# Block rounds of a two-layer decoder: inverses from ScalarE's logarithm and exponential, tables inside the first round, and new orders of smaller pieces

## The chip, the core and the metric

The kernel is one program on one core of a Trainium2 chip. Its engines run side by side and meet at semaphores: TensorE (PE; its weight loads are shown as PEld), VectorE (DVE), ScalarE (ACT), GpSimd (POOL), and SyncE, whose queue (SPq) starts most of the DMAs. The metric is the device time of one execution in microseconds (us).

## What is computed

The input is 64 sequences of 64 tokens with 256 channels, so 4096 tokens. Two layers follow each other; each has an attention part, a part that reads a context, and a feed-forward part. The change lies in the second and third part of layer 0:

```python
x = x + _L0_xattn_ref(64, 64, 256, L0_xattn_w, L0_xattn_u, _layernorm(x, axis=-1), ctx_2048)
x = x + _L0_ffn_ref(_layernorm(x, axis=-1), router_weight, router_bias, gate_up_proj, ...)   # 8 experts, best 2
```

The first of them is a recurrence over time in every channel, with key k (the normalised x) and value v (the context). Up to a common factor it is

```python
q_t = decay * q_(t-1) + exp(k_t);  p_t = decay * p_(t-1) + exp(k_t) * v_t      # decay = exp(w)
y_t = (p_(t-1) + exp(u + k_t) * v_t) / (q_(t-1) + exp(u + k_t))
```

The second normalises again, computes 8 logits per token, takes the best two, and sends the token to these two experts. The normalisation is (x - mean) / sqrt(variance + 1e-5), so every token needs the power -1/2 of a number, and every token and channel of the recurrence needs the inverse of a denominator.

## The kernel before

The kernel has four stages after each other: the linear attention of layer 0; the block rounds, which are changed here; the experts' matmuls over sorted rows; and layer 1. The block rounds and the experts are the function `recurrence_and_experts`.

**Blocks and rounds.** The 4096 tokens are 8 blocks of 512. A block goes through three steps, called f, y and r in the code. In step f its x is normalised (statistics on DVE, power -1/2 on POOL, scaling on ACT), TensorE turns keys and values to channels by time and adds the age of each time step from a small table (`aged`, `now`), and ACT takes the exponentials: `eh` of the keys, `fk` of the keys with the bonus u. POOL multiplies `eh` by the values `vt` (`ev`, function `weighted`). In step y DVE runs two scans with the decays `keep` (`qp` over `eh`, `pp` over `ev`), forms the denominator `den`, inverts it, and multiplies it by the numerator `num`, which POOL makes (functions `now_weighted`, line 1025, and `numerator`, line 1011). TensorE also makes key and value rows of the context for layer 1 (`cross_kv`, four tiles for each block, taken out by `kv_out` on ACT). In step r y is turned back and added to x (`residual`), normalised a second time (`xh`), and routed: logits, best two, their ranks in the experts' lists (`choose`, `place`), and POOL sends the rows out by indirect DMA (`scatter`, eight DMAs for each block). Weights of the experts are split into a high and a low part on the way (`weights_high` on ACT, `weights_low` on DVE, `down_high` on ACT, `down_low` on POOL).

Round i works on f of block i, y of block i-1 and r of block i-2, so there are 10 rounds (0 to 9), and rounds 2 to 7 hold all three steps. Each engine has the order of its pieces written out by hand, in a loop over `STEPS`; an engine does its pieces in that order and waits at a piece until its semaphores have come. On DVE the order is: statistics of f, `weights_low`, the router's weights of the block before, residual and statistics of r, both scans, the reciprocal (line 1412, `nc.vector.reciprocal(den[:], den[:])`), `choose`, the quotient (line 1417), `place`. On TensorE it is: tile 2 of `cross_kv` (y), `y_T` (r), tile 3 (y), `v_T` and `k_T` (f), `h_T` (r), tile 0 (f), `router` (r), tile 1 (f), `ranks` (r). In front of the loop DVE makes the tables `keep`, `aged`, `now`, and only then it starts on block 0.

**The power -1/2** is a function of POOL:

```python
def power(k, b):
    pool.wait_ge(S(f"var{k}"), 2 * b + 2)
    nc.gpsimd.tensor_tensor(out=rs[k][:], in0=ve[k][:], in1=neghalf[:], op=ALU.pow).then_inc(S(f"rs{k}"), 1)
    pool.wait_ge(S(f"rs{k}"), b + 1)
    nc.gpsimd.tensor_tensor(out=nm[k][:], in0=ng[k][:], in1=rs[k][:], op=ALU.mult).then_inc(S(f"nm{k}"), 1)
```

**After the rounds** DVE makes the table of the experts' tiles (`tile_table`), POOL sends the last block's rows, and the experts' stage begins when these have landed.

Of the kernel before, what the change touches and what calls it, by code (L numbers as in the profile page):

```python
# [11 lines left out]
P = 128  # L12
# [6 lines left out]
BT = 4  # L19
# [766 lines left out]
def recurrence_and_experts(nc, new_sem, x_sb, ident, slots, wts, rows, outs, bias_rows, gu_parts, w_gu, w_down, b_experts, w_router, b_router,  # L786
# [9 lines left out]
    BOUND = 60.0  # L796
    SEG = SEQ + 1
    NS = DC * BLK // SEQ
    I2 = 2 * D
    with ExitStack() as ctx:  # L800
# [17 lines left out]
        neghalf, iota, start_at = sb("neghalf", [P, BT]), sb("iota", [P, E]), sb("start_at", [P, E])  # L818
# [26 lines left out]
        with ExitStack() as rounds:  # L845
# [6 lines left out]
            den, num = own("den", [P, NS, SEQ]), own("num", [P, NS, SEQ])  # L852
# [3 lines left out]
        with ExitStack() as tiles:  # L856
# [24 lines left out]
            STEPS = [(i if i < BLOCKS else None, i - 1 if 1 <= i <= BLOCKS else None, i - 2 if i >= 2 else None) for i in range(BLOCKS + 2)]  # L881

            @block.sync
            def _(sp):
# [25 lines left out]
                sp.wait_ge(S("const"), 14)  # L910
# [63 lines left out]
            def _(pool):  # L974
                made = [nc.gpsimd.memset(neghalf[:], -0.5),
                        nc.gpsimd.iota(iota[:], [[1, E]], base=0, channel_multiplier=0, allow_small_or_imprecise_dtypes=True),
# [9 lines left out]
                pool.wait_ge(S("const"), 14)  # L986
# [12 lines left out]

                def power(k, b):  # L1000
                    pool.wait_ge(S(f"var{k}"), 2 * b + 2)
                    nc.gpsimd.tensor_tensor(out=rs[k][:], in0=ve[k][:], in1=neghalf[:], op=ALU.pow).then_inc(S(f"rs{k}"), 1)
                    pool.wait_ge(S(f"rs{k}"), b + 1)
                    nc.gpsimd.tensor_tensor(out=nm[k][:], in0=ng[k][:], in1=rs[k][:], op=ALU.mult).then_inc(S(f"nm{k}"), 1)
# [22 lines left out]
                def scatter(b, part=slice(0, 2 * BT)):  # L1027
                    pool.wait_ge(S("slot"), b + 1)
                    pool.wait_ge(S("xh"), 4 * b + 4)
                    for j, k in [divmod(n, 2) for n in range(2 * BT)][part]:  # L1030
                        nc.gpsimd.indirect_dma_start(
                            rows[:, :], bass.IndirectOffsetOnAxis(ap=sent_to[:, b * BT + j, k:k + 1], axis=0),
                            xh[b % 2][:, j, :], None).then_inc(S("sent1" if b % 2 else "sent"), 16)

                def down_low(n):
                    experts = slice(n * E // 4, (n + 1) * E // 4)
# [55 lines left out]
            def _(pe):  # L1092
# [9 lines left out]
                def k_T(b):  # L1102

                    for bank, table, done, read in ((TK, aged, "kT", "eh"), (TF, now, "fT", "fk")):
                        if b:
                            pe.wait_ge(S(read), b)
# [7 lines left out]
                        last.then_inc(S(done), 1)  # L1114

# [36 lines left out]
                def cross_kv(b, tiles):  # L1152

                    pe.wait_ge(S("vt"), b + 1)
                    if b == 0:
                        pe.wait_ge(S("kv_w"), 32)
                    for j in tiles:
# [6 lines left out]
                        last.then_inc(S("kvp"), 1)  # L1164

                pe.wait_ge(S("w_in"), 48)
                pe.wait_ge(S("const"), 15)
                pe.wait_ge(S("tab"), 11)
                for f, y, r in STEPS:
                    if y is not None:  # L1170
                        cross_kv(y, (2,))
                    if r is not None:
                        y_T(r)
                    if y is not None:
                        cross_kv(y, (3,))
                    if f is not None:
                        v_T(f)
                        k_T(f)
                    if r is not None:
                        h_T(r)  # L1180
                    if f is not None:
                        cross_kv(f, (0,))
                    if r is not None:
                        router(r)
                    if f is not None:
                        cross_kv(f, (1,))
# [1342 lines left out]
```

## Time and profile before

| | us |
|---|---|
| median of three timed runs | 3037.05 |
| lowest and highest of them | 3026.90, 3042.49 |
| the profiled execution, its own time | 3033.89 |
| its span, first to last instruction | 3032.2 |
| of it: linear attention, until | 1480.8 |
| block rounds, until the experts' first matmul | 1480.8 to 1738.3 |

The span is 1.7 us shorter than the execution's own time, which holds what lies before the first and after the last instruction. In a row of the trace, the times are microseconds from the start of the span, and what stands in brackets is how long the engine was idle just before and what ended that.

### The profile page before, as it was taken

The numbers are of one execution on the slowest core, as the hardware profiler recorded it, in microseconds if no ns is written. First come the engines' busy times: TensorE is split into PE (matmuls) and PEld (weight loads), VectorE is DVE, ScalarE is ACT, GpSimd is POOL, SyncE is SP. The second block draws the span as 40 slices with busy tenths as digits, with TensorE's granted clock in tenths as the row PEclk, the third lists the DMA queues.
The fourth block names the chain that finished last, engine by engine and source line by source line (L and its number), as shares of the span: only waits on it lengthen the run. The fifth ranks groups of instructions, "written<-read, shape, count | busy, mean of one in ns | idle before, by whom it ended". The sixth has DMA issues, their size and how long they took to land. (4 is left out here: it accounts for less than half of the span.)

```text
span 3032.2 us, 68140 instructions
## 1 busy us (share of the span) xinstructions
PE 2750.8 (91%) x22096; PEld 2295.9 (76%) x22128; DVE 2487.2 (82%) x5452; ACT 1954.2 (64%) x4120; POOL 2111.9 (70%) x2651
## 2 busy tenths in 40 slices
PE   6999999999999999999788499667999999999978
PEld 3888888888888888888555299535777777777767
DVE  6888888888888888888599577468899898989863
ACT  5888878778787877878444155346666666666642
POOL 5897666666666666666468544369888989898870
PEclk9999999999999999999899699768999999999989
DMA  4555444444444444444444399600000000000000
GB/s 144 172 193 169 133 143 139 144 135 146 137 131 153 131 143 132 155 131 128 142 152 146 134 337 333 207 15 18 20 19 27 21 25 24 22 24 22 21 5 11
DMA packets 185881, 340.09 MB, mean 112 GB/s; under 512 B 40668, under 2 KB 104037, under 8 KB 178936
## 3 DMA queue, kind: packets, MB, share of 16 engines
q1 hardware_dynamic: 179448, 319.55, 32.6%
q0 software_dynamic: 6144, 16.79, 1.8%
q8 instruction: 169, 2.77, 0.4%
q14 instruction: 120, 0.98, 0.1%
HBM read 264.68 MB, written 63.19 MB: 108 GB/s over the span
## 5 line engine op out<-in xcount | busy, mean ns | idle before, releaser
L1804 POOL TENSOR_TENSOR l_prod<-l_sco,l_kv 128x256 f32<-128x256 f32 x512 | 369.5, 760 | 36.4 <-DVE l_sco L2311 36.4
L1797 POOL TENSOR_TENSOR l_prod<-l_q,l_kv 128x256 f32<-128x256 f32 x512 | 358.9, 743 | 47.3 <-DVE l_att L2319 47.3
L718 DVE SCALAR_TENSOR_TENSOR a_cq<-a_PQ,a_taps,a_cq 128x504 f32<-128x504 f32 (+2 forms) x384 | 281.7, 734 | 72.7 <-ACT a_cq L584 63.6
L718 DVE SCALAR_TENSOR_TENSOR a_ck<-a_PK,a_taps,a_ck 128x504 f32<-128x504 f32 (+2 forms) x384 | 280.6, 731 | 9.7 <-ACT a_ck L584 0.5
L342 POOL TENSOR_TENSOR a_tq<-a_cq,a_tq 128x512 f32<-128x512 f32 x128 | 165.9, 1296 | 131.2 <-ACT a_tq L590 131.1
L329 POOL TENSOR_TENSOR a_hrs<-a_hve,a_neghalf 128x8 f32<-128x8 f32 x128 | 209.6, 1638 | 25.7 <-DVE a_hve L735 25.2
L485 PE MATMUL a_Y<-a_wo,a_og_parts 128*128 128x256 f32 x1536 | 205.9, 284 | 5.0 <-POOL a_og_parts L336 5.0
L412 PEld LDWEIGHTS a_X<-a_wv,a_xb 128*128 128x128 f32 x1536 | 200.0, 188 | 12.1 <-issue 1.2
L342 POOL TENSOR_TENSOR a_tk<-a_ck,a_tk 128x512 f32<-128x512 f32 x128 | 163.6, 1278 | 62.8 <-ACT a_tk L590 62.8
L412 PE MATMUL a_PQ<-a_x_hi,a_wqk 128*128 (+1 forms) x512 | 194.1, 420 | 12.6 <-issue 11.9
L412 PE MATMUL a_X<-a_wv,a_xb 128*128 128x256 f32 x1536 | 204.2, 282 | 0.8 <-DMA a_xb<-a_x_lo 0.8
L603 ACT ACTIVATE a_hk<-a_PK,a_lncol 128x512 f32<-128x512 f32 x128 | 99.9, 781 | 154.6 <-PE a_PK L504 154.6
L485 PEld LDWEIGHTS a_Y<-a_wo,a_og_parts 128*128 128x128 f32 x1536 | 194.7, 192 | 6.0 <-issue 5.9
L597 ACT ACTIVATE a_nq<-a_TQ,a_hnb,a_hrs 128x128 f32<-128x128 f32 x512 | 192.5, 463 | 1.5 <-POOL a_hnb L332 1.0
L597 ACT ACTIVATE a_nk<-a_TK,a_hnb,a_hrs 128x128 f32<-128x128 f32 x512 | 191.5, 457 | 0.0
L412 PE MATMUL a_X<-a_x_hi,a_wg 128*128 (+1 forms) x512 | 183.5, 399 | 2.3 <-DVE a_og L743 2.3
L412 PE MATMUL a_PK<-a_x_hi,a_wqk 128*128 (+1 forms) x512 | 182.6, 397 | 0.0
L336 POOL TENSOR_TENSOR a_og_parts<-a_og,a_og_parts 128x512 fp32r<-128x512 f32 x128 | 166.7, 1302 | 17.6 <-ACT a_og_parts L610 17.6
L584 ACT ACTIVATE a_cq<-a_PQ,a_taps 128x512 f32<-128x512 f32 x128 | 99.9, 780 | 100.0 <-PE a_PQ L412 100.0
L325 POOL TENSOR_TENSOR a_hm<-a_hst 128x8 f32<-128x8 f32 x128 | 26.7, 209 | 191.9 <-DVE a_hst L724 191.9
L772 DVE TENSOR_TENSOR_SCAN a_em<-a_dr,a_dm 128x256 f32<-128x256 f32 x128 | 160.0, 1250 | 0.0
L2319 DVE TENSOR_REDUCE l_att<-l_prod 128x64 f32<-128x1024 f32 x128 | 151.7, 1206 | 8.2 <-POOL l_prod L1804 8.0
(398 smaller groups left out, 8380.6 us busy)
## 6 DMA issues: line engine op xcount, KB each, us to landing
a_wqk<-qk_parts SPq DMA_DIRECT2D x112, 512.0 KB, 3.4
m_wgu<-gate_up_parts SPq DMA_DIRECT2D x39, 1024.0 KB, 8.1
a_wv<-v_parts SPq DMA_DIRECT2D x56, 512.0 KB, 3.8
a_wg<-g_parts SPq DMA_DIRECT2D x112, 256.0 KB, 3.3
a_wo<-o_parts SPq DMA_DIRECT2D x112, 256.0 KB, 2.9
a_dr<-decays SPq DMA_DIRECT2D x256, 64.0 KB, 2.6
m_hs<-sorted_rows SPq DMA_DIRECT2D x39, 256.0 KB, 7.1
sorted_outs<-m_ys SPq DMA_DIRECT2D x39, 256.0 KB, 7.5
```

Of the source, the lines that this page charges most:

```text
L329: nc.gpsimd.tensor_tensor(out=hrs[q][:], in0=hve[q][:], in1=neghalf[:], op=ALU.pow).then_inc(s_hrstd, 1)
L336: nc.gpsimd.tensor_tensor(out=og_parts[q][:, 1, :], in0=og[q][:], in1=og_parts[q][:, 0, :].bitcast(F32), op=ALU.subtract).then_inc(og_lo, 1)
L342: nc.gpsimd.tensor_tensor(out=t[i][p][:], in0=c[i][p][:], in1=t[i][p][:], op=ALU.mult).then_inc(s_silu, 1)
L412: last = nc.tensor.matmul(out, lhs(i, k), rhs(j, k), start=at_pass == PASSES[0], stop=at_pass == PASSES[-1])
L485: last = nc.tensor.matmul(Y[:, j, :], og_parts[p][:, i, j * P:(j + 1) * P], wo[p][:, w, :], start=first and j % 2 == 0 and k == 0, stop=Tr ...
L584: nc.scalar.activation(c[i][p][:], PB[i][:], ACT.Identity, bias=taps[p][:, bias:bias + 1], scale=taps[p][:, tap + KW - 1:tap + KW]).then_i ...
L597: nc.scalar.activation(nrm[i][q][:, j, :], TB[i][:, j, :], ACT.Identity, bias=hnb[q][:, k:k + 1], scale=hrs[q][:, k:k + 1]).then_inc(s_nor ...
L718: nc.vector.scalar_tensor_tensor(out=acc, in0=src, scalar=taps[p][:, tap + k:tap + k + 1], in1=acc, op0=ALU.mult, op1=ALU.add).then_inc(s_ ...
L772: nc.vector.tensor_tensor_scan(out=flat(em[q]), data0=flat(dr[q]), data1=flat(dm[q]), initial=0.0, op0=ALU.mult, op1=ALU.add).then_inc(s_e ...
L1797: nc.gpsimd.tensor_tensor(out=prod[:, h], in0=qv[:, h:h + 1, :].to_broadcast([P, H, HD]), in1=kk, op=ALU.mult).then_inc(S("E_pqk"), 1)
L1804: nc.gpsimd.tensor_tensor(out=prod[:, h], in0=sco[:, h:h + 1, :].to_broadcast([P, HD, H]), in1=vv, op=ALU.mult).then_inc(S("E_pav"), 1)
L2319: nc.vector.reduce_sum(att[:].rearrange("p (h d) -> p h d", d=HD)[:, 4 * k:4 * k + 4, :], prod[:, 4 * k:4 * k + 4], axis=AX).then_inc(S("E ...
```

## The change

The inverse of the denominator was one DVE reciprocal. Now DVE makes a first guess from the bits of the number (`guess`: an integer is taken from a constant), multiplies the denominator by it (`left`, close to 1), ACT takes the logarithm (`log`) and the exponential of its negative (`rest`), and DVE multiplies by the guess (`reciprocal`). The power -1/2 goes from POOL to ACT (`power`: logarithm and exponential; `shift`: four one-column copies). The tables are made inside round 0, behind the statistics of block 0. The work of an engine is cut into smaller pieces, a fourth step s (one round after r) takes the scatter and the router's weights, and each engine has a new order, written as a list of (step, piece). The round's index is again the block of f.

```diff
+            ROUND = dict(f=0, y=1, r=2, s=3)
+            def rounds(pieces):
+                for i in range(BLOCKS + max(ROUND.values())):
+                    for stage, piece in pieces:
+                        b = i - ROUND[stage]
+                        if 0 <= b < BLOCKS:
+                            piece(b)
...
 POOL
-                for f, y, r in STEPS:
-                    if r:
-                        scatter(r - 1, slice(0, 2))
-                    if f is not None:
-                        power(0, f)
-                    if y is not None:
-                        now_weighted(y)
-                    if r:
-                        scatter(r - 1, slice(2, 4))
-                    if r is not None:
-                        power(1, r)
-                    if y is not None:
-                        numerator(y)
-                    if f is not None:
-                        weighted(f)
-                    if r:
-                        scatter(r - 1, slice(4, 2 * BT))
-                    if r is not None and r < 4:
-                        down_low(r)
-                scatter(BLOCKS - 1)
+                rounds([("r", down_low), ("y", now_weighted), ("s", scatter(2, 4)), ("y", numerator), ("s", scatter(6, 8)), ("s", scatter(4, 6)),
+                        ("f", weighted), ("s", scatter(0, 2))])
...
 TensorE
+                rounds([("r", y_T), ("y", cross_kv(2)), ("y", cross_kv(3)), ("f", k_T(0)), ("r", h_T), ("f", v_T), ("r", router), ("f", k_T(1)),
+                        ("r", ranks), ("f", cross_kv(0)), ("f", cross_kv(1))])
...
 ACT
+                def power(k):
+                        nc.scalar.activation(rs[k][:], ve[k][:], ACT.Ln).then_inc(S(f"ln{k}"), 1)
+                        nc.scalar.activation(rs[k][:], rs[k][:], ACT.Exp, scale=-0.5).then_inc(S(f"rs{k}"), 1)
+                def shift(k):
+                        for j in range(BT):
+                            last = nc.scalar.activation(nm[k][:, j:j + 1], ng[k][:, j:j + 1], ACT.Copy, scale=rs[k][:, j:j + 1])
+                def log(b):
+                    act.wait_ge(S("left"), b + 1)
+                    nc.scalar.activation(den[:], den[:], ACT.Ln).then_inc(S("log"), 1)
+                def rest(b):
+                    nc.scalar.activation(den[:], den[:], ACT.Exp, scale=-1.0).then_inc(S("rest"), 1)
+                nc.scalar.preload_act_table_set("natural_log_exp_and_others")
+                rounds([("f", power(0)), ("f", shift(0)), ("f", keys_in), ("f", decays), ("y", kv_out(2)), ("r", power(1)), ("r", shift(1)),
+                        ("r", rows_out), ("y", kv_out(3)), ("r", h_out), ("y", log), ("y", rest), ("f", v_out), ("f", k_out), ("f", weights_high),
+                        ("f", now_out), ("r", odds), ("f", kv_out(0)), ("y", down_high), ("f", kv_out(1))])
...
 DVE
+                def guess(b):
+                    nc.vector.tensor_scalar(near[:].bitcast(I32), den[:].bitcast(I32), -1.0, INVERSE_BITS, ALU.mult, ALU.add).then_inc(S("near"), 1)
+                def left(b):
+                    nc.vector.tensor_tensor(out=den[:], in0=den[:], in1=near[:], op=ALU.mult).then_inc(S("left"), 1)
                 def reciprocal(b):
-                    nc.vector.reciprocal(den[:], den[:]).then_inc(S("rec"), 1)
+                    nc.vector.tensor_tensor(out=den[:], in0=den[:], in1=near[:], op=ALU.mult).then_inc(S("rec"), 1)
...
+                rounds([("f", statistics(0)), ("f", moments(0)), ("f", variance(0)), ("y", sums), ("r", residual), ("r", statistics(1)),
+                        ("f", tables), ("r", moments(1)), ("r", variance(1)), ("y", denominator), ("y", value_sums), ("y", guess), ("s", shares),
+                        ("y", left), ("y", weights_low), ("r", choose), ("r", best), ("r", numbers), ("r", one_hot), ("y", reciprocal), ("r", pairs),
+                        ("y", quotient), ("r", place), ("r", pick), ("r", slot), ("r", gap)])
```

`sums` is the scan `qp`, `value_sums` the scan `pp`, `keys_in` and `rows_out` the two scalings, `shares` the router's weights, `place`, `pick` and `slot` together the old `place`. `tables` and `decays` do something in round 0 only, `down_low` and `down_high` for four blocks only.

## Rows read from the trace of the kernel before

**Rows 1.** Busy time of each engine by stretch: the block rounds, one full round

```profile
core 0: us, PE busy (x) PEld busy (x) DVE busy (x) ACT busy (x) POOL busy (x), PEclk, DMA share, GB/s
1481.00:1735.00 254.00, 186.64 (x912) 117.07 (x912) 200.15 (x457) 96.88 (x150) 171.36 (x145) 0.84 0.45 157
1558.00:1584.00 26.00, 22.25 (x115) 13.86 (x114) 23.12 (x53) 12.40 (x19) 20.26 (x16) 0.93 0.40 148
```

**Rows 2.** Timeline of DVE: first instructions of rounds 3 to 8, waits for the router

```profile
1545.72 1.40 DVE L1377 BATCH_NORM_STATS2 m_st<-x_sb 128x6 f32<-128x256 f32 x4
...
1628.20 1.40 DVE L1377 BATCH_NORM_STATS2 m_st<-x_sb 128x6 f32<-128x256 f32 x4
...
1648.29 0.19 DVE L1421 TENSOR_TENSOR m_lg<-m_TY,m_rb 128x32 f32<-128x32 f32 x1 [0.85 <-PE m_TY L1138]
...
1652.12 1.40 DVE L1377 BATCH_NORM_STATS2 m_st<-x_sb 128x6 f32<-128x256 f32 x4
...
1679.02 1.22 DVE L1472 TENSOR_TENSOR m_wgu<-m_raw_gu,m_wgu 128x1024 fp32r<-128x1024 f32 x1
```

**Rows 3.** Groups of DVE by line in the block rounds: busy, mean ns, idle

```profile
L1412 DVE RECIPROCAL m_den<-m_den 128x1024 f32<-128x1024 f32 x8 | 52.2, 6524 | 0.0
...
L1417 DVE TENSOR_TENSOR m_num<-m_num,m_den 128x1024 f32<-128x1024 f32 x8 | 9.8, 1219 | 0.1
...
L1526 DVE TENSOR_SCALAR m_keep<-m_keep,m_wc 128x512 f32<-128x512 f32 x2 | 0.9, 480 | 0.0
```

**Rows 4.** Groups of ACT by line in the block rounds

```profile
L1266 ACT ACTIVATE m_eh<-m_TK 128x1024 f32<-128x1024 f32 x8 | 8.1, 1009 | 3.9 <-PE m_TK L1112 3.9
...
L1281 ACT ACTIVATE m_te<-m_te 128x4 f32<-128x4 f32 x8 | 1.6, 201 | 12.2 <-DVE m_te L1431 12.2
L1303 ACT ACT_TABLE_LOAD x1 | 1.3, 1283 | 7.3 <-PEq L2412 7.3
```

**Rows 5.** One line of layer 1: four-byte columns scaled by ACT

```profile
L2062 ACT ACTIVATE l_nmD<-l_rsD,l_ngD x32: 280/295/295, 1950.7 to 2843.9; 128x1 f32<-128x1 f32 x32
```

**Rows 6.** Groups of POOL by line in the block rounds

```profile
L1031 POOL DMA_INDIRECT sorted_rows<-m_xh,m_sent_to x64 | 72.0, 1126 | 40.8 <-DVE m_sent_to L1468 25.1 <-issue 15.5 <-ACT m_xh L1258 0.2
L1002 POOL TENSOR_TENSOR m_rs<-m_ve,m_neghalf 128x4 f32<-128x4 f32 x16 | 23.2, 1450 | 11.8 <-DVE m_ng L1385 11.5
L1025 POOL TENSOR_TENSOR m_fv<-m_fk,m_vt 128x1024 f32<-128x1024 f32 x8 | 18.8, 2351 | 0.2 <-ACT m_fk L1271 0.2
L1018 POOL TENSOR_TENSOR m_ev<-m_eh,m_vt 128x1024 f32<-128x1024 f32 x8 | 17.4, 2178 | 10.7 <-ACT m_eh L1266 10.7
L1004 POOL TENSOR_TENSOR m_nm<-m_ng,m_rs 128x4 f32<-128x4 f32 x16 | 8.7, 544 | 1.3
```

**Rows 7.** Timelines of POOL and DVE: both at work together, one after the other

```profile
1523.11 2.36 POOL L1025 TENSOR_TENSOR m_fv<-m_fk,m_vt 128x1024 f32<-128x1024 f32 x1
...
1568.85 2.35 POOL L1038 TENSOR_TENSOR m_wd_low<-m_wd_low,m_wd_high 128x1024 fp32r<-128x1024 f32 x1
...
1558.67 2.17 POOL L1011 TENSOR_TENSOR m_num<-m_fv,m_pp 128x1024 f32<-128x1024 f32 x1
...
1523.73 2.82 DVE L1472 TENSOR_TENSOR m_wgu<-m_raw_gu,m_wgu 128x1024 fp32r<-128x1024 f32 x1 [1.95 <-ACT m_wgu L1295]
...
1568.57 2.66 DVE L1431 TENSOR_TENSOR m_te<-m_mx 128x4 f32<-128x4 f32 x1
...
1558.46 6.52 DVE L1412 RECIPROCAL m_den<-m_den 128x1024 f32<-128x1024 f32 x1
```

**Rows 8.** Timelines of ACT and DVE: the start, the end, the experts' first tanh

```profile
1495.58 1.02 ACT L1266 ACTIVATE m_eh<-m_TK 128x1024 f32<-128x1024 f32 x1 [1.42 <-PE m_TK L1112]
...
1505.12 1.22 DVE L1472 TENSOR_TENSOR m_wgu<-m_raw_gu,m_wgu 128x1024 fp32r<-128x1024 f32 x1 [9.74 <-ACT m_wgu L1295]
...
1703.09 0.17 DVE L1468 CAST m_sent_to<-m_row_of 128x8 uint32<-128x8 f32 x1
...
1747.88 0.63 ACT L1344 ACTIVATE m_th<-m_gp 128x512 f32<-128x512 f32 x1 [3.07 <-DVE m_gp L1571]
```

More of the change, by code:

```diff
@@ L1025, in now_weighted, with scatter, piece @@
                     nc.gpsimd.tensor_tensor(out=fv[:], in0=fk[:], in1=vt[:], op=ALU.mult).then_inc(S("fv"), 1)
[L1027 to L1033, printed above, removed]
+                def scatter(start, stop):
+                    def piece(b):
+                        pool.wait_ge(S("slot"), b + 1)
+                        pool.wait_ge(S("xh"), 4 * b + 4)
+                        for j, k in [divmod(n, 2) for n in range(start, stop)]:
+                            nc.gpsimd.indirect_dma_start(
+                                rows[:, :], bass.IndirectOffsetOnAxis(ap=sent_to[:, b * BT + j, k:k + 1], axis=0),
+                                xh[b % 2][:, j, :], None).then_inc(S("sent1" if b % 2 else "sent"), 16)
+                    return piece
                 def down_low(n):
+                    if n >= 4:
+                        return
                     experts = slice(n * E // 4, (n + 1) * E // 4)
@@ L1100, in v_T, with k_T, piece @@
                     last.then_inc(S("vT"), 1)
-                def k_T(b):
-                    for bank, table, done, read in ((TK, aged, "kT", "eh"), (TF, now, "fT", "fk")):
-                        if b:
+                def k_T(n):
+                    bank, table, done, read = ((TK, aged, "kT", "eh"), (TF, now, "fT", "fk"))[n]
+                    def piece(b):
+                        if b == 0:
+                            pe.wait_ge(S("w_in"), 48)
+                            pe.wait_ge(S("const"), 14)
+                            pe.wait_ge(S("tab"), 11)
+                        else:
                             pe.wait_ge(S(read), b)
@@ L1524, in _ @@
-                for c in range(DC):
-                    v = keep[:, c * (NS // DC):(c + 1) * (NS // DC), 1:SEG]
-                    nc.vector.tensor_scalar(v, v, wc[:, 0, c:c + 1], None, ALU.add).then_inc(S("tab"), 1)
-                for c in range(DC):
-                    nc.vector.tensor_scalar(aged[:, c, :], aged[:, c, :], wc[:, 1, c:c + 1], None, ALU.mult).then_inc(S("tab"), 1)
-                dve.wait_ge(S("tab"), 7)
-                for c in range(DC):
-                    nc.vector.tensor_scalar(now[:, c, :], aged[:, c, :], wc[:, 2, c:c + 1], BOUND, ALU.add, ALU.min).then_inc(S("tab"), 1)
@@ L1532, in _, with tables @@
[L1532 to L1554 removed]
+                def tables(b):
+                    if b:
+                        return
+                    dve.wait_ge(S("w_in"), 48)
+                    dve.wait_ge(S("const"), 14)
+                    nc.vector.tensor_scalar(wc[:, 0, :], wuc[:, 0:DC], 0.0, None, ALU.min).then_inc(S("tab"), 1)
+                    nc.vector.tensor_scalar(wc[:, 1, :], wuc[:, 0:DC], 0.0, -1.0, ALU.max, ALU.mult).then_inc(S("tab"), 1)
+                    dve.wait_ge(S("tab"), 2)
+                    nc.vector.tensor_tensor(out=wc[:, 2, :], in0=wuc[:, DC:2 * DC], in1=wc[:, 1, :], op=ALU.subtract).then_inc(S("tab"), 1)
+                    for c in range(DC):
+                        v = keep[:, c * (NS // DC):(c + 1) * (NS // DC), 1:SEG]
+                        nc.vector.tensor_scalar(v, v, wc[:, 0, c:c + 1], None, ALU.add).then_inc(S("tab"), 1)
+                    for c in range(DC):
+                        nc.vector.tensor_scalar(aged[:, c, :], aged[:, c, :], wc[:, 1, c:c + 1], None, ALU.mult).then_inc(S("tab"), 1)
+                    dve.wait_ge(S("tab"), 7)
+                    for c in range(DC):
+                        nc.vector.tensor_scalar(now[:, c, :], aged[:, c, :], wc[:, 2, c:c + 1], BOUND, ALU.add, ALU.min).then_inc(S("tab"), 1)
+                    dve.wait_ge(S("tab"), 9)
+                    for c in range(DC):
+                        nc.vector.tensor_scalar(now[:, c, :], now[:, c, :], -BOUND, None, ALU.max).then_inc(S("tab"), 1)
```

213 lines of the change are left out of this document (93 added, 120 removed).

## Prediction

> **What bounds the kernel now.** I read the stages first, then the block rounds by engine, then one round instruction by instruction. The change touches only the block rounds, 254 of 3032 us. In them DVE is busy 200.2 us, TensorE 186.6, POOL 171.4 and ACT 96.9; in one full round of 26.0 us DVE has 23.1 and TensorE 22.3 [rows 1]. So DVE comes first, and TensorE close behind it. The five full rounds 3 to 7 take 133.3 us, from 1545.72 to 1679.02. The round from 1628.20 to 1652.12 shows what DVE needs when almost nothing disturbs it: 23.9 us, of which 0.85 went to waiting for the router, so 23.1 us of work [rows 2]. The rest of the mean of 26.7 is waits for the router and, in three rounds, a stall that decides this case.
>
> **The stall.** DVE and POOL do not always run side by side. `weights_low` takes 1.2 us alone; started 0.6 us after POOL's `now_weighted` it took 2.82, and ended 1.1 us after it. A subtraction of four elements took 2.66 us and ended when POOL's `down_low` did [rows 7]. Both DVE instructions read two tensors from SBUF, as POOL's do. While DVE ran the reciprocal, which reads one, POOL's `numerator` started 0.2 us after it and took its usual 2.17 us [rows 6, 7]. So the reciprocal, slow as it is, is the time in which POOL works without stopping DVE: 6.5 us in each round [rows 3], in which `numerator` and `weighted` (2.18 us [rows 6]) both fit.
> The Trainium skill has this as a rule: on the page "SBUF — State Buffer", section "Who interferes with whom", a DVE instruction with two SBUF inputs contends with a GpSimd instruction that reads SBUF, and the later one blocks fully. The rows agree. By the same section a `tensor_scalar` in a two-port mode contends too, so that `guess` would keep `numerator` waiting; were `guess` free of it, I estimate the sum below lower by 0.8 us in each of five rounds, 4 us. No row here shows `guess`.
>
> **The change, part by part, for one full round.**
> *DVE work.* The reciprocal goes, 6.5 us. `guess` comes: 1024 elements by a `tensor_scalar`. The nearest row has 512 in 0.48 us, so it lies between 0.8 and 1.2 (the price of a two-input instruction of that size); I take 0.8, since it has one input like its row. `left` and the new `reciprocal` come, two-input products of 1024 elements at 1.2 us [rows 3]. The rest is cut and put in another order, but the instructions are the same. 23.1 - 6.5 + 0.8 + 2.4 = 19.8 us.
> *What POOL now stops.* `numerator` waits for the second scan, as before. Behind the scan now stand `guess`, the router's weights, `left` and `weights_low`, all but a few elements of them two-input work: `numerator` gets its turn behind `guess`, and DVE stands for its 2.2 us. `weighted` waits for `eh`. In the new order of ACT this comes after `log`, `rest` and `v_out`: four instructions of 1.0 us [rows 4] and some 0.1 between them, 4.4 us after `left`. At that moment DVE is in the quotient (`weights_low`, the choice, `reciprocal` and quotient are 1.2 + 1.7 + 1.2 + 1.2 us, the choice by its place in the round), and `pick` behind it waits: 2.0 us. Then come two scatters, each 0.96 to 1.13 us and 0.3 between [rows 6], and `now_weighted`, 2.5 us after `weighted` has ended. By then DVE has done `pick`, `slot` and the first statistics, some 2.4 us, and wants to start its first scan. Who is first is a matter of 0.1 us. The four-element row started 0.3 us before POOL's instruction and lost all the same [rows 7], so I let POOL win: 2.3 us. If DVE wins, the cost is nothing, since the residual and the statistics of r read one SBUF tensor each and cover it. In three of the five rounds `down_low` (2.35 us [rows 7]) stands in front of `now_weighted`. I take nothing for it, because DVE, kept waiting by it, then gets to its scan first and `now_weighted` goes under the statistics; if POOL keeps its turn, it is the full 2.35.
> So a round takes 19.8 + 2.2 + 2.0 + 2.3 = 26.3 us, and five take 131.5. The bounds are 5 x 24.0 = 120 (`now_weighted` and `down_low` cost nothing) and 131.5 + 3 x 2.35 = 138.6. Against 133.3 this is -1.8 us, between -13.3 and +5.3.
> *TensorE* keeps its work. At 22.3 us it fits under 26.3, and its pieces for the router end before DVE asks for them, so the waits for the router (0.85 in the row shown) should go. *POOL* loses both powers, (23.2 + 8.7) / 8 = 4.0 us a round [rows 6]; its 20.3 become 16.3. *ACT* gets two instructions of 1.0 us, four small ones of 0.2 and eight one-column copies of 0.3 [rows 4, 5]: 12.4 + 6.0 = 18.4 us, under 26.3. From the variance to the first scaled tile it is two small ones and four copies, 1.5 us, where POOL took 1.45 + 0.54: no gain on the path, as this chain is covered by the scans.
> *The start.* Before, DVE stood 9.74 us in front of `weights_low`, while `eh` of block 0 had been there since 1496.6; the first scan began at 1506.3 [rows 8]. Now `weights_low` stands behind the scans, and the scan can start with `eh`, 9.7 us earlier. In exchange `weighted` and `now_weighted` of block 0, which ran in that wait, fall between the scans: -9.7 + 2.2 + 2.35 = -5 us, with bounds -9.7 and 0 (TensorE has the same work before block 0's router). The statistics in front of the tables gain nothing of their own: TensorE waits for the tables in both.
> *The end.* Round 8 has no f; it took 24.2 us, from 1679.02 to 1703.2 [rows 2, 8]. The trade of the reciprocal gives -3.3 and `numerator` +2.2; the wait for a slow router shrinks by about 2: -3 us, between -1 and -5. Round 9 and the table of tiles stay.
> *The tables of ACT.* One load of 1.28 us [rows 4] at the start is replaced by another, and the experts' tanh needs one more. ACT has been idle for 3.07 us there [rows 8]: I take 0; without that cover 1.3.
> Sum: -1.8 - 5 - 3 = -9.8 us. The profiled execution took 3033.9, which gives 3024; the median of the runs lies 3.2 above it, so against that the gain shows as 13 us, 0.4%.
>
> **Rivals.**
> *The port costs little.* `now_weighted` and `down_low` fall under the statistics, the start gains more: -13.3 - 5 to -9.7 - 5, so 23 to 28 us, 3006 to 3011. For it speaks that one of the two stalls hangs on 0.1 us, against it that POOL won each time in the rows.
> *The change does all that its operations promise.* No stall at all; TensorE is the bound at 22.3 us [rows 1], five rounds take 111.3: -22 - 9.7 - 5, so about 2997. Against it stand the two stalls of rows 7; nothing in the trace shows two-input work of both engines together at full speed.
> *The port takes everything.* `down_low` costs in full: -2.7 us, 3031.
> *Slower: ACT reloads its tables.* Logarithm and exponential alternate six times a round (three pairs). If each change loads a table at 1.28 us [rows 4], ACT gets 7.7 us a round, 26.1 in all, and two or three loads stand on the chain from `left` over `log` and `rest` to `eh`: 2.6 to 3.9 us over 8 rounds, 21 to 31, less 9.8: about 3050. It decides from two loads a round on this chain. Before, one load served the whole stage [rows 4], but without a logarithm, so the rows leave it open.
> The Trainium skill, page "ScalarE: Activation LUTs", section "Table sets: the hidden batching unit", says that one set holds both functions. By that the loads stay at one; no run so far shows it.
>
> **How the numbers follow.** A measurement of this kernel can tell about 0.5%, 15 us, from no change; the three runs span as much. Chances: forecast 0.45 (its own range 3015 to 3033), port costs little 0.27, no stall 0.06, port takes everything 0.12, table loads 0.05, and 0.05 for a chain that I have not seen and that makes a round longer than 27.5 us. Under 3022 lie the second and third and 0.08 of the forecast: faster 0.41. The loads (3045 with two of them on the chain, 3055 with three) and the chain unseen I count as slower, over 3052: 0.10. The rest, 0.49, is within 0.5%. The range goes from 3003, below the cheap port, to 3043, half way to the loads.
>
> **What would show it.** In the profile after: `numerator`, `weighted` and `now_weighted` as POOL rows each with a DVE instruction of 2 us or more beside it that takes 0.2 to 1.2 alone; a first scan near 1497; rounds of about 26 us with no wait for the router; one or two table loads in the stage. I am wrong if rounds come to 22 to 24 us with these DVE rows at their usual lengths, or if table loads appear by the dozen.

## The result, and the profile after

Seven timed runs of each kernel gave a median of 3017.62 us after the change (3014.88 to 3028.24) and 3037.05 us before: ratio 0.9948, 95% interval 0.9925 to 0.9971. The change makes the kernel about 0.5% faster. The profiled execution took 3016.4 us by its own time (span 3014.7), where 3033.9 stood before and 3024 was forecast.

Where the 17.5 us of the span come from, by the two traces (the block rounds counted from POOL's first instruction in them to the start of the experts' first tanh):

| us | before | after | difference | forecast |
|---|---|---|---|---|
| linear attention, until the block rounds | 1480.8 | 1483.0 | +2.2 | 0 |
| start of the rounds, until round 3 | 64.9 | 59.7 | -5.2 | -5 |
| rounds 3 to 7 | 133.3 | 127.6 | -5.7 | -1.8 |
| round 8 | 24.2 | 19.4 | -4.8 | -3 |
| round 9 to the first tanh | 44.7 | 44.6 | -0.1 | 0 |
| experts and layer 1 | 1284.3 | 1280.5 | -3.8 | 0 |

The block rounds give 15.8 us, 267.1 before and 251.3 after. The first and last line of the table are code that no kernel here changes; over the 14 profiles of this study they lie between 1478.4 and 1490.0, and between 1279.9 and 1293.4. So one profile tells a difference inside the rounds far better than one in the total, and the experiments below are read by the rounds first. Their start has a spread of its own: in the eight profiles whose code is the same up to the first scan (changed, and runs 1, 3, 4, 5, 6, 8 and 10 below) this scan begins 15.3 to 17.6 us after the start of the rounds, and the changed kernel, with 17.2, lies near the top. A difference of 2 us over all the rounds can be that alone.

Busy time by stretch of the changed kernel, for all the rounds and for one round (answers to [rows 1]):

```profile
1483.00:1722.00 239.00, 189.80 (x912) 117.14 (x912) 202.96 (x473) 132.56 (x262) 157.41 (x114) 0.85 0.48 167
1567.00:1592.00 25.00, 23.52 (x118) 13.80 (x118) 24.41 (x59) 16.70 (x33) 22.06 (x13) 0.97 0.50 175
```

DVE is as busy as before (203 us against 200) though the reciprocals, 52 us, are gone. Its groups by line say what filled the place (answers to [rows 3]; busy, mean ns, idle before):

```profile
L1431 DVE TENSOR_TENSOR_SCAN m_pp<-m_keep,m_ev 128x1040 f32<-128x1040 f32 x8 | 20.7, 2583 | 0.0
L1417 DVE TENSOR_TENSOR_SCAN m_qp<-m_keep,m_eh 128x1040 f32<-128x1040 f32 x8 | 18.5, 2316 | 7.6 <-ACT m_eh L1274 7.6
L1493 DVE TENSOR_SCALAR m_te<-m_te 128x4 f32<-128x4 f32 x8 | 14.3, 1790 | 0.0
L1401 DVE TENSOR_SCALAR m_ve<-m_mv 128x4 f32<-128x4 f32 x16 | 14.1, 881 | 1.6
```

Two groups that work on four columns take 28 us: the first instruction of the router's weights (L1493) and the variance (L1401). They are not slow, they stand. The timeline of DVE has three of them in round 7, with the start of each:

```profile
1647.77 1.59 DVE L1401 TENSOR_SCALAR m_ve<-m_mv 128x4 f32<-128x4 f32 x1
...
1658.21 0.67 DVE L1436 TENSOR_SCALAR m_near<-m_den 128x1024 int32<-128x1024 int32 x1
1658.80 2.14 DVE L1493 TENSOR_SCALAR m_te<-m_te 128x4 f32<-128x4 f32 x1
...
1667.81 1.98 DVE L1511 TENSOR_TENSOR m_picked<-m_oh,m_rank 128x64 f32<-128x64 f32 x1
```

and the timeline of POOL has the product beside each (`now_weighted`, `numerator`, `weighted`; answers to [rows 7]):

```profile
1646.97 2.35 POOL L1027 TENSOR_TENSOR m_fv<-m_fk,m_vt 128x1024 f32<-128x1024 f32 x1
...
1658.44 2.47 POOL L1013 TENSOR_TENSOR m_num<-m_fv,m_pp 128x1024 f32<-128x1024 f32 x1 [4.69 <-ACT m_xh L1255]
...
1666.58 3.13 POOL L1020 TENSOR_TENSOR m_ev<-m_eh,m_vt 128x1024 f32<-128x1024 f32 x1 [0.72 <-ACT m_eh L1274]
```

Each DVE row ends within 0.1 us of the product's end. In the five full rounds 15 such rows take 33.2 us and would take 0.17 us each alone: 6.1 us a round stand at the port, where the prediction had 6.5. The dearest is in round 5, where POOL went from `down_low` straight to `now_weighted` and DVE stood through both (POOL, then DVE):

```profile
1593.82 2.35 POOL L1045 TENSOR_TENSOR m_wd_low<-m_wd_low,m_wd_high 128x1024 fp32r<-128x1024 f32 x1
1596.13 2.35 POOL L1027 TENSOR_TENSOR m_fv<-m_fk,m_vt 128x1024 f32<-128x1024 f32 x1
```

```profile
1593.81 4.70 DVE L1401 TENSOR_SCALAR m_ve<-m_mv 128x4 f32<-128x4 f32 x1
```

On ACT, by line, the new work is cheap, and of table loads there are two, at the start of the rounds and ahead of the experts' tanh (answers to [rows 4]):

```profile
L1248 ACT ACTIVATE m_nm<-m_ng,m_rs 128x1 f32<-128x1 f32 x64 | 13.6, 283 | 0.5
L1291 ACT ACTIVATE m_den<-m_den 128x1024 f32<-128x1024 f32 x8 | 8.5, 1058 | 19.1 <-DVE m_den L1440 19.1
...
L1325 ACT ACT_TABLE_LOAD x1 | 1.3, 1283 | 7.3 <-PEq L2451 7.3
L1347 ACT ACT_TABLE_LOAD x1 | 1.3, 1283 | 0.0
```

The first scan, on DVE's timeline, now waits for `eh` and for nothing of the weights (answers to [rows 8]):

```profile
1500.18 2.33 DVE L1417 TENSOR_TENSOR_SCAN m_qp<-m_keep,m_eh 128x1040 f32<-128x1040 f32 x1 [7.59 <-ACT m_eh L1274]
```

### The profile page after: what moved, and what is told of

Its sections match the earlier page's. It is cut to its first block and busy times, and to the rows that moved or that the text cites. A ratio compares the mean times of both kernels' runs of the same rounds, so it can differ in the third digit from the quotient of the medians.

```text
span 3014.7 us, 68300 instructions
## 1 busy us (share of the span) xinstructions
PE 2755.2 (91%) x22096; PEld 2297.8 (76%) x22128; DVE 2487.1 (83%) x5468; ACT 1990.4 (66%) x4233; POOL 2099.5 (70%) x2618
## 5 line engine op out<-in xcount | busy, mean ns | idle before, releaser
L412 PEld LDWEIGHTS a_X<-a_wv,a_xb 128*128 128x128 f32 x1536 | 199.8, 188 | 12.1 <-issue 1.2
```

The source lines that it names most:

```text
L412: last = nc.tensor.matmul(out, lhs(i, k), rhs(j, k), start=at_pass == PASSES[0], stop=at_pass == PASSES[-1])
```

## The experiments

Times from the start of the block rounds, in us, each from one profile; the ratio is to the kernel before, timed beside each run (its medians lay between 3032.6 and 3038.9). Run 6 leaves most of the numerators out.

| kernel | median | ratio, 95% interval | first scan | rounds 3 to 7 | all rounds |
|---|---|---|---|---|---|
| before | 3037.05 | | 25.4 | 133.3 | 267.1 |
| changed | 3017.62 | 0.9948 (0.9925 to 0.9971) | 17.2 | 127.6 | 251.3 |
| 1 inverse undone | 3043.40 | 1.0019 (1.0005 to 1.0033) | 15.9 | 135.9 | 268.2 |
| 2 products on DVE | 3012.26 | 0.9912 (0.9897 to 0.9926) | 20.6 | 118.3 | 241.5 |
| 3 `now_weighted` after the scan | 3013.11 | 0.9917 (0.9905 to 0.9930) | 15.4 | 121.9 | 243.7 |
| 4 `numerator` later | 3024.17 | 0.9949 (0.9938 to 0.9961) | 15.4 | 128.4 | 251.6 |
| 5 products on DVE, two moved | 3007.35 | 0.9902 (0.9883 to 0.9920) | 15.4 | 115.7 | 240.4 |
| 6 products cut | 3001.57 | 0.9875 (0.9857 to 0.9893) | 15.5 | 109.4 | 231.5 |
| 7 start undone | 3035.31 | 0.9993 (0.9977 to 1.0008) | 22.9 | 133.8 | 265.4 |
| 8 one product on POOL, placed | 3005.70 | 0.9887 (0.9867 to 0.9906) | 17.6 | 111.8 | 236.4 |
| 9 only tables first | 3021.86 | 0.9964 (0.9948 to 0.9979) | 19.5 | 131.3 | 259.0 |
| 10 reciprocal as cover | 3021.24 | 0.9964 (0.9948 to 0.9979) | 15.3 | 124.0 | 250.4 |
| 11 power on POOL | 3048.82 | 1.0055 (1.0035 to 1.0075) | 16.2 | 148.1 | 273.7 |
| 12 before, power on ACT | 3037.98 | 1.0009 (0.9994 to 1.0024) | 25.4 | 134.9 | 269.7 |

**Is the port the loss?** Run 6 takes POOL's products away (nearly), and its quotient reads `fv` in the place of `num`; run 2 gives the products to DVE.

```diff
 POOL, all three products
-  out=num[:], in0=fv[:], in1=pp[:, :, 0:SEQ]
+  few = slice(0, NS if b < 2 else 1)
+  out=num[:, few], in0=fv[:, few], in1=pp[:, few, 0:SEQ]
...
```

> The changed kernel with POOL's three products cut to a sixteenth of their columns from block 2 on (the quotient reads the stale product of now_weighted, so most of the numerators are left out). Theory (the port): the DVE rows of 2 us and more beside the products go back to 0.1 to 0.2 us, except for down_low's; DVE then has 19.2 us of work, and TensorE with 22.3 is the next bound: rounds of 22.3 to 23, waits of DVE for the router come back at 2 to 3 us a round, the stage loses about 16 us against the 251.3 as changed. Rival 1 (the long rows come from something other than these products, DVE's own queue or the scatters): they stay, rounds of 24.4 and more. Rival 2 (TensorE is no bound): rounds of 19.5 to 20.5.

In rounds 3 to 7 no DVE row but the scans takes over 1.45 us: the long rows came from the products. The rounds alternate between 21.4 and 22.6 us, mean 21.9, and DVE waits for the router in each of the eight rounds that have one: 1.6 to 1.7 us in each of rounds 3 to 7, and 17.8 in all, of which 8.5 are in the last round, where every kernel here waits 8.5 to 9.1. These are the rows of the choice's first line (instances and durations, then idle time before them), and the busy time of rounds 3 to 7 (PE first, granted clock 0.97):

```profile
L1457 DVE TENSOR_TENSOR m_lg<-m_TY,m_rb x8: 191/192/193, 1538.8 to 1689.3; 128x32 f32<-128x32 f32 x8
...
  PE m_TY L1137: 17.8, 8
```

```profile
1545.29:1654.72 109.43, 108.22 (x572) 68.45 (x571) 95.43 (x278) 81.11 (x163) 66.23 (x57) 0.97 0.50 177
```

TensorE is busy for 108.2 of 109.4 us, so it is the next bound. The rounds lose 19.8 us, where 16 was expected. Of the 6.1 us a round that stood at the port, 3.6 come back (25.5 to 21.9); the rest turns into waits for TensorE.

```diff
 POOL
-  rounds([("r", down_low), ("y", now_weighted), ("s", scatter(2, 4)), ("y", numerator), ("s", scatter(6, 8)), ("s", scatter(4, 6)),
-          ("f", weighted), ("s", scatter(0, 2))])
+  rounds([("r", down_low), ("s", scatter(2, 4)), ("s", scatter(6, 8)), ("s", scatter(4, 6)), ("s", scatter(0, 2))])
 DVE
+  ... ("r", variance(1)), ("y", now_weighted), ("y", denominator) ... ("y", left), ("y", numerator) ... ("y", quotient), ("f", weighted) ...
```

> The changed kernel with POOL's three products (numerator, weighted, now_weighted) on DVE, 1.22 us each. Theory (the port): 3.66 us more work on DVE, but no stall except down_low's: 19.2 + 3.7 = 22.9 us a round in place of 25.5, so 2.6 less in each of 8: about 2998. Rival 1 (another chain, TensorE's or the router's, sets the round and the stalls only fill its slack): rounds stay at 24.4 or more, the shortest as changed, 3010 to 3017, with new waits of DVE for the router. Rival 2 (POOL's products do run beside DVE for most of their time): 8 x 3.66 = 29 us longer, 3046.

DVE does 3.66 us more a round and the rounds 3 to 7 are 9.3 us shorter in sum: 22.8 to 23.1 us, as expected, but 24.9 twice, where `down_low` stopped the variance (rows of 2.28 and 1.93 us). All the rounds gained 9.8 us and not 8 x 2.6 = 21. Those two rounds account for 4 of what is missing; the rounds at both ends gave next to nothing (0.7 before round 3, -0.2 after round 7). There the first scan comes 3.3 us later than as changed, since `weighted`, which waits for `eh`, kept the statistics of block 1 behind it; that this is the whole reason is not shown.

**Placing the products.** Run 3 lays `now_weighted` under work that does not stop; run 4 tries that with `numerator`.

```diff
 now_weighted
+  pool.wait_ge(S("qscan"), b + 1)
-  rounds([("r", down_low), ("y", now_weighted), ...
+  rounds([("y", now_weighted), ("r", down_low), ...
```

> The changed kernel, with now_weighted waiting for the end of the first scan of its block, and down_low behind it. Theory (the port): now_weighted then falls under residual and the statistics of r and stops nobody; the rows of 1.5 to 2.4 us on the variance go back to 0.17: 1.3 to 2.2 us less in each round from 2 to 8, 4 in the round with down_low, less what down_low now costs the denominator (up to 1.5 in three rounds): about 8 us less, 3009. Rival (another chain sets the round): the same us appear as waits of DVE for the router, 3015 to 3018.

7.6 us less over the rounds, as expected, though 1.9 of them lie before the first scan, where the edit changes nothing (15.4 against 17.2); rounds 3 to 7 give 5.7. With one wait more, POOL's product lies under the residual and the statistics of r. In POOL's and DVE's timelines:

```profile
1574.66 2.35 POOL L1028 TENSOR_TENSOR m_fv<-m_fk,m_vt 128x1024 f32<-128x1024 f32 x1 [2.73 <-DVE m_qp L1418]
```

```profile
1574.34 1.26 DVE L1410 TENSOR_TENSOR x_sb<-m_TY,x_sb 128x512 f32<-128x512 f32 x2
1575.52 1.39 DVE L1385 BATCH_NORM_STATS2 m_st<-x_sb 128x6 f32<-128x256 f32 x4
```

The residual's and the statistics' rows keep their length beside it. `down_low`, which now follows `now_weighted`, stops the variance of r instead, for 1.6 to 1.7 us in each of the rounds 3 to 5.

```diff
 numerator
+  pool.wait_ge(S("w_low"), b + 1)
-  ("y", numerator), ("s", scatter(6, 8)), ("s", scatter(4, 6)), ("f", weighted)
+  ("s", scatter(6, 8)), ("s", scatter(4, 6)), ("y", numerator), ("f", weighted)
```

> The changed kernel, with numerator waiting for weights_low, two pairs of scatters in front of it. Theory (the port): numerator then runs under choose, best and numbers, which read PSUM or one SBUF tensor; the 2.1 us row on the shares goes back to 0.16, at most 0.4 is lost at one_hot: 1.7 us less in each of 8 rounds, 13 us: 3004. Rival (another chain sets the round, or the stall only moves to the reciprocal's second product): 3015 to 3018.

No gain over the rounds, where 13 us were forecast. The long row on the shares did go (0.23 us), but three losses took its place. In two rounds the quotient waited 3.0 us for `num` and then stood beside `weighted`, which came right behind `numerator`; scatters that took 1.96 and 1.54 us in front of it, in the place of 0.96, are half of that wait. In a third round `weighted` stopped the second product (3.20 us). And DVE now asks for the router 7 us after the variance of r instead of 9, while TensorE has it ready after 7.0 to 9.4, so that DVE waits for it in every round: 6.2 us in rounds 3 to 7, against 0.6 as changed. On DVE's timeline:

```profile
1569.87 3.12 DVE L1450 TENSOR_TENSOR m_num<-m_num,m_den 128x1024 f32<-128x1024 f32 x1 [3.04 <-POOL m_num L1014]
...
1593.97 0.19 DVE L1454 TENSOR_TENSOR m_lg<-m_TY,m_rb 128x32 f32<-128x32 f32 x1 [1.41 <-PE m_TY L1134]
```

So both halves of the rival happened: the stall moved, and the router's chain showed beneath it. Part of the 2 us beside `numerator` is time in which DVE would otherwise wait for the router.

**Undoing the inverse alone.**

```diff
 DVE
-  ("y", value_sums), ("y", guess), ("s", shares), ("y", left), ("y", weights_low) ... ("y", reciprocal), ("r", pairs)
+  ("y", value_sums), ("y", reciprocal), ("s", shares), ("y", weights_low) ... ("r", pairs)
+  nc.vector.reciprocal(den[:], den[:])
 ACT
-  ("r", h_out), ("y", log), ("y", rest), ("f", v_out)
+  ("r", h_out), ("f", v_out)
```

> The changed kernel with the old inverse: one reciprocal on DVE in the place of guess; left, the second product, log and rest go. All else as changed. Theory (what the inverse saves on DVE is given back at the SBUF port): DVE's own work goes from 19.2 to 19.2 - 0.66 - 2.44 + 6.52 = 22.6 us a round, but numerator lies under the reciprocal and stops nobody; with now_weighted's 1.5 to 2.3 and half of weighted's 1.8 a round takes 25.0 to 25.8, against a mean of 25.5 as changed: 3012 to 3024. Rival (the inverse is worth its operations, 3.4 us a round): 8 x 3.4 = 27 us longer, 3045.

17 us longer, between the two theories. Rounds 3 and 4 take 25.0 and 25.1 us, as the first theory had it, and the reciprocal covered `numerator`. But in rounds 6 and 7, of 28.2 and 30.1 us, `weighted`, four DMAs of `scatter` behind `numerator`, came just after the reciprocal had ended, and `now_weighted` before the quotient, so two stalls stayed and grew (DVE's rows of round 6):

```profile
1646.09 2.78 DVE L1498 TENSOR_TENSOR wts<-wts,m_te 128x4 f32<-128x4 f32 x1
...
1651.69 2.90 DVE L1484 TENSOR_TENSOR m_both<-m_oh 128x32 bf16<-128x32 f32 x1
```

Run 10 mends just that:

```diff
 POOL, on top of run 1
+  down_low one round later, behind wait_ge(S("gap"), n + 1); now_weighted behind wait_ge(S("qscan"), b + 1)
+  rounds([("s", down_low), ("y", now_weighted), ("s", scatter(2, 4)), ("y", numerator), ("f", weighted), ("s", scatter(6, 8)),
+          ("s", scatter(4, 6)), ("s", scatter(0, 2))])
```

> The old inverse, one reciprocal, but with POOL's products laid under what does not stop DVE: numerator and weighted back to back under the reciprocal, now_weighted behind the first scan, down_low a round later under the statistics of f. Theory (most of the loss is at the port, with either inverse): DVE has 22.6 us of work and no stall, 22.6 to 23.5 a round in place of 28 in the later rounds of the first run with the reciprocal; the stage takes 240 to 247 against the 251.3 as changed and 268 there, so it beats the change without the new inverse: about 3010. Rival (the inverse is worth its 3.4 us a round whatever the order): 26 us more than the best kernel with the new inverse (236), so 262 or longer, 3030.

250.4 us: the old reciprocal, with the products under it, is as good in the rounds as the whole change (1.9 us less before round 3, 3.6 less in rounds 3 to 7, 4.6 more in rounds 8 and 9), and the two intervals of the ratio overlap. Two of the rounds 3 to 7 take 23.4 us; in the other three, scatters in front of `down_low` push it onto the variance and they take 25.8, which is why it missed the 240 to 247:

```profile
1561.54 3.06 DVE L1403 TENSOR_SCALAR m_ve<-m_mv 128x4 f32<-128x4 f32 x1
```

This does not make the new inverse worthless. With the products placed too (run 8 below) its rounds take 22.4 us in the place of the 23.4 of the two undisturbed ones here: of the 3.4 us that it saves DVE, 2.4 go to the two products that DVE then makes itself, and 1.0 is left.

**The start.**

```diff
 run 9
-  ("r", statistics(1)), ("f", tables), ("r", moments(1))
+  rounds([("f", tables), ("f", statistics(0)), ...
 run 7, besides
-  ("y", left), ("y", weights_low)
+  ("f", variance(0)), ("y", weights_low), ("y", sums)
```

> The changed kernel with the start undone: the tables in front of the statistics of block 0, and weights_low before the first scan in each round. Theory (the start was won by taking DVE's wait for ScalarE's weights out of the path of the first scan): the first scan starts some 25 us after the stage's start in place of 17, round 3 some 5 us later, and the stage takes 5 us more, 256; later rounds change by less than 1 us each, as DVE's work is the same. Rival (the start came from the statistics in front of the tables): the first scan is late by 2 us only.

> The changed kernel with the tables alone moved back in front of the statistics of block 0; weights_low stays behind the scans. Together with the run that undid both, this tells which half of the start counts. Theory (as predicted, the tables gain nothing of their own): first scan within 1.5 us of the 17.2 after the stage's start, stage 251 to 253. Rival (the statistics before the tables start the chain to the first eh earlier): first scan at 20 to 23, stage 254 to 257.

The first scan comes 2.3 us later with the tables in front, and 3.4 more with `weights_low` in front too; round 3 starts 2.3 and 7.0 us later. So most of the start is `weights_low`, but the tables' place is worth 2.3 us where nothing was expected (2 to 4, if the first scans at 15.3 to 17.6 are taken together). Run 7's theory that the later rounds keep their length failed: the stage took 265.4 us and not 256. It is 14.1 longer than as changed, 6.2 of that in rounds 3 to 7, where `now_weighted` met the first scan twice (rows of 4.47 us) and DVE waited 1.8 us for the router in every second round. In run 9 POOL's `down_low` and `now_weighted` met the variance back to back in two rounds instead of one (4.70 us each), and rounds 3 to 7 took 3.7 us more.

**The power -1/2.**

```diff
 run 11, changed kernel: POOL
+  rounds([("f", power(0)), ("r", down_low), ("y", now_weighted), ("s", scatter(2, 4)), ("r", power(1)), ("y", numerator), ...
 run 12, kernel before: ACT, in front of each scaling
+  activation(rs, ve, Ln); activation(rs, rs, Exp, scale=-0.5); 4 x activation(nm, ng, Copy, scale=rs)
```

> The changed kernel with the power -1/2 back on POOL, as before. Theory (as predicted, the move to ScalarE gains nothing on the path by itself): the chain from variance to the first scaled tile is 2.0 us on POOL and 1.4 on ScalarE, under the scans in both; the stage stays within 3 us of 251.3. Rival (the power on POOL reads two SBUF tensors and stops DVE, or waits behind DVE's scan): the first scan of a round is held or the power comes 2.3 us late; the keys of f and the rows of r come later by that, 1 to 3 us a round, stage 259 to 275.

> The kernel before, with one part of the change alone: the power -1/2 of both normalisations on ScalarE (logarithm, exponential, four one-column copies), in front of each scaling; all orders, the reciprocal and the start as before. Theory (my step was wrong: on POOL the power of r waits behind a scatter and DVE's scan, 6.0 us from the variance to the first scaled tile, and that is what makes the router late): xh comes some 4 us earlier, DVE's waits for the router, 12.8 us in rounds 3 to 8, go, and the stage takes 253 to 259 in place of 267.1; 3023 to 3030. Rival 1 (as predicted, the move gains nothing on the path): 264 to 268. Rival 2 (POOL, with its queue freed, starts now_weighted and numerator earlier and stops DVE's residual, scan or weights_low for longer): router waits go, but DVE rows of 2 us and more take their place, 264 or longer.

Run 11 is 22.4 us longer and DVE waits for the router in every round, 41.8 us in all, where the changed kernel has 9.4 (8.5 of it in the last round). The reason stands in its timeline of POOL: the power of r waits behind `down_low`, `now_weighted` and two scatters. That place in POOL's order, near the one it had before, is my choice; another might cost less. Run 12, the same part alone in the kernel before, takes DVE's waits for the router away in rounds 3 to 8 (they were 12.8 us): from the variance of r to the router's end on TensorE it is 9.0 to 10.9 us, before 13.0 to 15.9, and DVE asks after 12.1. It gains nothing all the same, as its second rival said: POOL's products come earlier and stop DVE for longer, here `weights_low` beside `now_weighted` and the last cast beside `down_low`, on DVE's timeline of one round, with the choice's first row, which now waits for nothing:

```profile
1599.20 0.13 DVE L1426 TENSOR_TENSOR m_lg<-m_TY,m_rb 128x32 f32<-128x32 f32 x1
...
1602.90 2.60 DVE L1473 CAST m_sent_to<-m_row_of 128x8 uint32<-128x8 f32 x1
...
1607.40 4.09 DVE L1477 TENSOR_TENSOR m_wgu<-m_raw_gu,m_wgu 128x1024 fp32r<-128x1024 f32 x1
```

**The best of them.** Run 5 moves `weighted` and `down_low` a round later on top of run 2; run 8 besides gives `now_weighted` back to POOL, behind the scan.

```diff
 run 5: DVE ("r", variance(1)), ("y", weighted), ("y", now_weighted), ("y", denominator); POOL ("s", down_low) behind wait_ge(S("qscan"), n + 3)
 run 8: DVE ("r", variance(1)), ("y", weighted), ("y", denominator); POOL ("s", down_low) behind wait_ge(S("gap"), n + 1),
        ("y", now_weighted) behind wait_ge(S("qscan"), b + 1), then the scatters; ACT's v_out waits for ev too
```

> The three products on DVE, and besides: weighted one round later, between the statistics of r and now_weighted, and down_low one round later, waiting for the end of the first scan. Theory (the port is the loss, and nothing else is near): against the run with the products on DVE alone, the two rounds of 24.8 us, in which down_low stopped the variance for 1.8 us, come to 22.9 as well, and the first scan, which stood behind weighted, comes 3 to 5 us earlier: 6 to 9 us less from the stage's start to the experts' first tanh, 233 to 236 in place of 241.5 (251.3 as changed). In time some 3004. Rival (TensorE is the bound now, or weighted on its later place holds the second scan): rounds of 24 and more, 241 or longer.

> As the kernel with the products on DVE and weighted a round later, but now_weighted stays on POOL and waits for the end of the first scan, and down_low, a round later, waits for the last piece of DVE's round, so that it lies under the statistics of f. Theory: DVE has 1.2 us less work a round, 21.7; TensorE's 22.3 comes first, so 22.3 to 22.7 a round, 2 to 4 us less over the stage than with all three on DVE, with waits for the router of some 0.5 us a round. Rival 1 (port): down_low overlaps the variance by 0.4 and more, or now_weighted reaches into the denominator: no gain, rounds of 23. Rival 2 (TensorE is no bound): 21.7 to 22.0 a round, 8 us less.

Run 5 has full rounds of 22.7 to 24.1 us; it gains 1.1 over all the rounds and not 6 to 9, because rounds 8 and 9 took back 3.1 of the 4.1 gained until then. Run 8 has rounds of 22.1 to 22.7, and TensorE is busy almost throughout (busy time in a stretch of 112 us; PE first, DVE third):

```profile
1545.00:1657.00 112.00, 110.14 (x572) 69.52 (x571) 107.87 (x287) 82.40 (x164) 76.73 (x49) 0.95 0.52 183
```

At 3005.7 us it beats both kernels, by 1.1% against the one before; its interval lies below the changed kernel's.

## Why the prediction was right, point by point

**The time** came out within its range, 7.6 us under the forecast, on the profile's own time. Of these 3.9 are in rounds 3 to 7, 1.8 in round 8, 0.2 in the start, and 1.7 elsewhere: 0.1 in round 9, the rest where nothing changed. The median, 0.52% below the old one, falls just beyond the prediction's line of 0.5%: in the outcome to which it gave 0.41, not in the one with 0.49.

**DVE's work**, forecast at 19.8 us a round, is 19.2 to 19.5 (a round less what its long rows lose and, in round 6, 0.8 us of waits). `guess` took 0.66 us, not 0.8.

**The three stalls** are there as named. `numerator` cost 2.0 to 2.3 us (forecast 2.2), `weighted` 1.8 to 2.0 (2.0). For `now_weighted` I let POOL win the 0.1 us; it cost 1.3 to 2.2 in each of the five rounds, but not always in that way. In rounds 6 and 7 it stops the variance in front of the first scan, as DVE came later into it than I had it. In rounds 3 and 4 DVE's scan came first, as I had it, but it was `down_low` that the scan held and that went under the statistics, and `now_weighted` behind it stopped the variance of r (POOL, then DVE, round 3):

```profile
1545.16 4.03 POOL L1045 TENSOR_TENSOR m_wd_low<-m_wd_low,m_wd_high 128x1024 fp32r<-128x1024 f32 x1 [4.50 <-ACT m_wd_high L1323]
1549.15 2.36 POOL L1027 TENSOR_TENSOR m_fv<-m_fk,m_vt 128x1024 f32<-128x1024 f32 x1
```

```profile
1544.72 2.31 DVE L1417 TENSOR_TENSOR_SCAN m_qp<-m_keep,m_eh 128x1040 f32<-128x1040 f32 x1
...
1550.05 1.49 DVE L1401 TENSOR_SCALAR m_ve<-m_mv 128x4 f32<-128x4 f32 x1
```

So `down_low`, taken at nothing, cost nothing in two of its three rounds and 2.3 in the third (round 5, above): the bound of the rival in which the port takes everything, but once only. 19.4 + 6.1 makes the 25.5 us of a round. On the Trainium skill's page "SBUF — State Buffer", section "Who interferes with whom", a `tensor_scalar` can run in a two-port mode and then contends with GpSimd; the trace agrees, `numerator` took 2.47 to 2.48 us when it began 0.2 us into `guess` (rounds 5 to 7), 2.18 when it began behind it (rounds 3 and 4), and 2.17 beside the reciprocal [rows 7]. Where the prediction says that the rows agree that the later one blocks, they agree on what contends, not on the order: its four-element row started 0.3 us ahead of `down_low` and stood [rows 7], and so, by 0.01 us, did the row of 4.70 above.

**ACT**'s sum has a slip that decides nothing: two of 1.0, four of 0.2 and eight of 0.3 us make 5.2, not 6.0; it was busy for 4.6 us more a round.

**TensorE** was put at 22.3 us, below the round. Run 6 shows the floor at 21.9, and run 8 reaches 22.4. So the rival without stalls named the next bound rightly; the change as written doesn't reach it, since the stalls stay.

**The step that failed is "no gain on the path" for the power.** I compared durations, 1.5 us on ACT and 2.0 on POOL, and left out what POOL's instruction waits for: before, in the round from 1573.66, the variance of r was written at 1580.44 to 1580.72 and `xh` began at 1586.55, 5.8 us later, behind two scatters and DVE's scan. After, it is 1.5 us (1629.27 to 1630.73). That kept the router late, and by runs 11 and 12 its end, not slack on TensorE, is why DVE's waits for the router went. The sum came out all the same, because it had these waits at nothing for another reason: that part is luck. POOL's timeline of before has the wait in it:

```profile
1581.88 1.83 POOL L1031 DMA_INDIRECT sorted_rows<-m_xh,m_sent_to  x1 [0.30 <-issue]
1583.73 1.38 POOL L1002 TENSOR_TENSOR m_rs<-m_ve,m_neghalf 128x4 f32<-128x4 f32 x1
1585.18 1.25 POOL L1004 TENSOR_TENSOR m_nm<-m_ng,m_rs 128x4 f32<-128x4 f32 x1
```

The power begins only as the scatter ends, 3.0 us after the variance.

**The start** came as summed, -5.2, in part by luck, since its terms did not. The first scan came 8.2 us earlier, not 9.7, as the first `eh` began 1.3 us later than before (16.2 against 14.8 us after the start). Undone in the changed kernel, `weights_low` is worth 3.4 us at the first scan and 4.7 at round 3. That the statistics ahead of the tables gain nothing was wrong by 2.3 us there (run 9); against the kernel before, which had its `eh` no later, no gain of theirs is to be seen. **Round 8** gained 4.8 in place of 3. **The tables:** one load serves every logarithm and exponential and one more stands ahead of the tanh, whose input came 1.8 us after it; no cost, and the rival with reloads is out. The Trainium skill's page "ScalarE: Activation LUTs", section "Table sets: the hidden batching unit", has both functions in one set; the trace agrees with two loads.

**What the parts are worth** can't be added: undone alone, the inverse costs 16.9 us of the rounds, the start 14.1, the power 22.4, and all of them together are worth 15.8. Each makes a new meeting of POOL and DVE when it moves alone. What stays open is how an order with the power on POOL at a better place would do; it wasn't tried.

## What to carry to other kernels

Before a slow instruction is taken off an engine, ask what runs in its shade: here 6.5 us of reciprocal hid two products of another engine, and a reciprocal with the products laid under it was as good as the new inverse without such placing. With it, the new inverse was better by 1.0 us a round, not by the 3.4 of its operations. Two engines that stop each other are planned like one: either lay the other's work under what does not stop, by a wait for the right event, or give it to the engine that would stand anyway (1.2 us of work in place of 2 us of standing). Expect only a part of a stall back: beneath it lie the waits for the next engine. And cost a moved step from when its input is ready to when its reader starts, not by its duration.

## What was not expected of the hardware

A DVE instruction that was already waiting for POOL's `down_low` also stood through the next POOL instruction, which followed without a gap: 4.70 us for 2.35 + 2.35, and twice more in run 9. A `scatter` takes 0.96 us alone, 1.96 beside `weights_low` and up to 3.16 beside DVE's first scan and the residual (run 2), while the scan beside it keeps its 2.31 to 2.33 us: the delay goes one way, and it is half of what made run 4's `numerator` late.
